# Two buffers instead of three for the transposed probabilities, four instead of two for the x tiles

## The reference, cut to what matters

```
h = max(layernorm(x), 0)
q = h @ Wq + bq;  k = h @ Wk + bk;  v = h @ Wv + bv        (8 heads of 64)
scores = q k^T / 8 + (adj == 0 ? -1e9 : 0)
x = x + softmax(scores) @ v
```

## Time and profile before

| | before |
|---|---|
| median of 3 runs | 4067.93 us (4066.05 to 4071.46) |
| the profiled execution | 4066.34 us |
| its span, first to last instruction | 4064.5 us |
| granted TensorE clock, mean | 0.999 |
| busy: PE / DVE / ACT / POOL | 4017.7 / 3064.8 / 3077.6 / 1401.6 us |
| batches x slots | 16 x 128 = 2048 |
| a slot, on average | 4064.5 / 2048 = 1.98 us |

### The profile page before, as it was taken

The page is one execution under the profiler, slowest core; times in us unless marked ns, Lnnn a source line. Parts: engine busy times, 40 slices in busy tenths (PEclk is TensorE's granted clock), DMA queues, the critical chain, the costliest instruction groups (busy, mean ns, idle before and its releaser), DMA issues. The chain is left out here.

```text
span 4064.5 us, 64393 instructions
## 1 busy us (share of the span) xinstructions
PE 4017.7 (99%) x22016; PEld 3277.6 (81%) x22016; DVE 3064.8 (75%) x5128; ACT 3077.6 (76%) x5514; POOL 1401.6 (34%) x1409
## 2 busy tenths in 40 slices
PE   7999999999999999999999999999999999999998
PEld 6888888888888888888888888888888888888886
DVE  6877867777777777777777687776877868768686
ACT  5877868778687786877868688686886868868687
POOL 4333333333333333333333333333333333333322
PEclk9999999999999999999999999999999999999999
DMA  5232223222223232222222232222322313223121
GB/s 183 69 93 63 85 59 84 86 65 83 70 72 86 66 85 80 62 83 80 74 81 64 78 92 61 81 79 64 93 66 77 85 59 91 83 59 98 38 73 47
DMA packets 239955, 314.83 MB, mean 77 GB/s; under 512 B 16401, under 2 KB 147473, under 8 KB 231057
## 3 DMA queue, kind: packets, MB, share of 16 engines
q1 hardware_dynamic: 239632, 310.71, 26.8%
HBM read 172.23 MB, written 37.75 MB: 52 GB/s over the span
## 5 line engine op out<-in xcount | busy, mean ns | idle before, releaser
L830 DVE TENSOR_TENSOR pT<-T,pT 128x512 fp32r<-128x512 f32 x2048 | 1390.7, 688 | 750.2 <-ACT pT L665 733.4
L665 ACT CAST pT<-T 128x512 fp32r<-128x512 f32 x2048 | 1186.1, 591 | 656.4 <-PE T L546 575.4
L824 DVE CUSTOM_DVE_ANT_0 S<-S,mask 128x1024 f32<-128x1024 f32 x1024 | 1252.1, 1223 | 3.1 <-PE S L535 3.1
L546 PE MATMUL T<-ident,probs 128*128 128x128 f32 x8192 | 1231.8, 273 | 1.0 <-ACT probs L673 0.6
L546 PEld LDWEIGHTS T<-ident,probs 128*128 128x128 f32 x8192 | 1006.6, 140 | 277.7 <-DVE pT L830 41.4
L673 ACT ACTIVATE probs<-S,negmax 128x1024 f32<-128x1024 f32 x1024 | 1151.5, 1124 | 8.4 <-DVE negmax L824 5.2
L565 PE MATMUL O<-pT,vs 128*64 128x512 f32 x2048 | 964.5, 471 | 0.2 <-DVE pT L830 0.2
L558 PE MATMUL O<-pT,vs 128*128 128x512 f32 x2048 | 816.1, 398 | 0.0
L504 PE MATMUL misc<-hT,wqk 128*128 128x512 f32 x3036 | 787.4, 395 | 7.7 <-ACT y L656 7.7
L504 PEld LDWEIGHTS misc<-hT,wqk 128*128 128x128 f32 x3036 | 556.9, 188 | 160.7 <-issue 42.9
L409 POOL TENSOR_TENSOR outs<-outs,oT 64x512 f32<-64x512 f32 x256 | 336.1, 1313 | 562.4 <-DMA outs<-oT 556.2
(11 more groups left out here) (70 smaller groups left out, 3587.5 us busy)
## 6 DMA issues: line engine op xcount, KB each, us to landing
wqk<-wqk_split SPq DMA_DIRECT2D x63, 1024.0 KB, 7.1
xln<-in_x SPq DMA_DIRECT2D x240, 256.0 KB, 2.7
outs<-in_x SPq DMA_DIRECT2D x66, 512.0 KB, 4.8
kA<-kA SPq DMA_DIRECT2D x128, 256.0 KB, 3.2
kB<-kB SPq DMA_DIRECT2D x128, 256.0 KB, 3.8
outs<-oT SPq DMA_DIRECT2D x256, 128.0 KB, 3.1
out<-outs SPq DMA_DIRECT2D x64, 512.0 KB, 4.4
probs<-in_adj SPq DMA_DIRECT2D x4, 1024.0 KB, 5.0
```

The lines of the kernel that those rows point to most:

```text
L546: mm = pe.transpose(T[:, u % 2, i * P:(i + 1) * P], probs[:, (GB * g + i) % RING, j * P:(j + 1) * P], ident[:])
L665: act.copy(pT[:, u % PT, 0, :], T[:, u % 2, :]).then_inc(p_hi, 1)
L824: dve.tensor_tensor_reduce(S[:, s % 2, :], S[:, s % 2, :], mask[:, s % NB, :], 1.0, 3.0e38, ALU.add, ALU.min, negmax[:, s % RING:s % RING ...
L830: dve.tensor_tensor(pT[:, u % PT, 1, :], T[:, u % 2, :], pT[:, u % PT, 0, :].bitcast(F32), ALU.subtract).then_inc(p_lo, 1)
```

## The change

`PT` goes from 3 to 2, so that pT has 8 KB a partition and not 12. `XLN` goes from 2 to 4, so that xln has 8 KB and not 4. With two buffers 128 is a multiple of the number of buffers, and the condition of `probs_hi` is the same in all slots: the `contract_lo` of u-2 must be done. No instruction is added or removed; the number of x loads is the same (16 a batch), four of them are issued at a batch's beginning and not two, and four and not six after transpositions.

```diff
-PT = 3
+PT = 2
...
-XLN = 2
+XLN = 4
 XLN_USES = [len(range(r, NB, XLN)) for r in range(XLN)]
...
                 n = UNITS * b + u
                 act.wait_ge(turned, n + 1)
 
-                used = n + 1 - (PT if u >= PT - 1 else PT - 1)
+                used = n + 1 - PT
                 if some(used):
                     act.wait_ge(contracted, used)
                 act.copy(pT[:, u % PT, 0, :], T[:, u % 2, :]).then_inc(p_hi, 1)
```

## The result

| | before | after |
|---|---|---|
| median | 4069.04 us (4066.05 to 4071.46) | 4323.23 us (4322.93 to 4324.79) |
| ratio, 95% interval | | 1.0626 (1.0607 to 1.0644): slower |
| span of the profiled execution | 4064.5 us | 4321.3 us |
| granted TensorE clock, mean | 0.999 | 0.999 |

The forecast was 4306 us, in a range of 4255 to 4400. By the spans (first to last instruction) the change cost 4321.3 - 4064.5 = 256.8 us; the sum had said 239.9.

What follows compares the result with a forecast made beforehand. PE, with only 12.7 us idle in its steady part, was taken to set the end. The terms 13.9 + 127.1 + 62.5 + 42.4 - 6 = 239.9 us, added to the profiled 4066.3 us, gave 4306 us, range 4255 to 4400.

Steps and rivals of the forecast that it cites:

- the sum: All terms of the forecast added up, four losses less the x tiles' gain: 239.9 us slower.
- The bound: PE's instruction list sets the end; it had 12.7 us idle, and a matmul that begins later is lost time.
- (b): Projections waiting for copy_y behind v = 10 and 2: PE stalls 1.65 or 1.33 us each, 127.1 + 62.5 us.
- (c): v = 18 and 26, no projection behind: the transposes two slots later start 0.53 us late in 80 places, 42.4 us.
- (a): Ordinary slots: probs_hi begins 0.29 us later, which costs only at the transposes of v = 17, 48 places, 13.9 us.
- Part 1, x tiles: Four x tiles end POOL's wait for loads; PE's waits at L483 shrink, a gain of 6 us, at most 15.0.
- the cover: At L483, most of a weight load's wait (10.4 us in all) is covered by the matmul beside it.
- The price of the wait: On ACT, probs_hi follows the end of the contract_lo it waits for by 0.09 us.
- The clock: Rival: PE's clock falls at the new gaps behind v = 2 and 10, up to 211 us more, 4517 us; chance 0.09.
- The loop without slack: Rival: the loop through ACT and DVE has no slack, so slots without fills lose 0.29 us, about 4636; chance 0.06.
- Not slower: Third rival: the wait is hidden at copy_y too and only the x tiles count, 4060 us; 0.04 with the fourth.

Runs made afterwards that it cites:

- experiment 1: The changed kernel with two x tile buffers (XLN = 2) in place of four: 4330.81 us, ratio to before 1.0644.
- experiment 4: The kernel before, with probs_hi waiting for contract_lo of u-2 in all slots but those with u mod 8 = 2: 4086.02 us, ratio 1.0041.
- experiment 3: The kernel before, with probs_hi's later wait only in slots with u mod 8 = 2 (and a batch's first two, as always): 4313.9 us, ratio 1.0602.
- experiment 5: The changed kernel, with ACT doing copy_y ahead of probs_hi in v = 2 and 10: 4135.18 us, ratio to before 1.016.
- experiment 7: The kernel before (three pT buffers, two x tiles), with copy_y between probs_hi and the exponential in v = 2 and 10: 4060.79 us, ratio 0.9981.

## Why the prediction was right, point by point

**The bound.** That PE's list sets the end held in every run: counted from the first instruction, the last matmul is 256.8 us late in the profile after, and the spans differ by 256.8; in each of the nine experiments' traces the two agree within 0.1 us too. The sum was 17.2 us short of 257.1: 7.7 in (b), 10.2 and 3.2 in places that it put at nothing and 0.2 in (c), less 2.1 in (a) and 2.0 at L483.

**Part 1, x tiles (-6 us).** The sign and the cover were right; the size was 8 us by matmul starts and 7.6 by medians of experiment 1. The step that was short is the cover of the weight loads' wait: PE's idle time came to 4.6 us in 8 places, but by matmul starts each of the 15 batches gained at L483, 0.2 to 1.9 us.

**The price of the wait (0.09 us).** It is 0.09 us again in the profile after, where `contract_lo` ends at 1965.72 and `probs_hi` begins at 1965.81.

**(a) Ordinary slots (13.9 us).** Measured 11.8 at v = 16 and 17, in the predicted pairs; experiment 4 has 12.0. But 7.2 of the 11.8 us stand one slot earlier than I said, at v = 16. The rows of after (ACT, DVE, PE):

```profile
1976.44 0.19 ACT L673 ACTIVATION_READ_ACCUMULATOR probs<-S,negmax 128x1 f32 x1
```

```profile
1975.99 0.66 DVE L830 TENSOR_TENSOR pT<-T,pT 128x512 fp32r<-128x512 f32 x1
```

```profile
1976.77 0.42 PEld L546 LDWEIGHTS T<-ident,probs 128*128 128x128 f32 x4 [0.39 <-ACT probs L673]
1976.80 0.63 PE L546 MATMUL T<-ident,probs 128*128 128x128 f32 x4
```

The transposes of v = 16 need both the exponential of v = 14, which ends at 1976.63, and `probs_low(14)`, which ends at 1976.65. Which of them is last can't be told from 0.02 us; the profile books the wait under the exponential, 40.9 us in 147 places, where it had 1.5 before. I had looked at `probs_low(15)` and v = 17 alone. The delay of 0.29 us is the same on all these ways, and what v = 16 takes, v = 17 need not take again, so the sum came out close all the same, in part by luck.

**(b) The projections (127.1 + 62.5 us).** Right in place, count and mechanism; experiments 3 and 5 show both. The term was mis-sized by 7.7 us of 189.6: v = 11 cost 1.75 us each and not 1.65. The first projection matmul is late by 1.67, as worked out. The rest is that the group itself lasts longer when it begins after a standstill: six matmuls show 1.62 us, and 1.54 when they follow without one. By the starts the difference lies between the first matmul and the second, 0.30 us apart and not 0.235; the cause is not shown. In the 47 places where the kernel before already waited, its group already showed 1.62, and there the term fits: 62.8 measured.

**(c) v = 20 and 28 (42.4 us).** Measured 42.6, but this is luck: two errors cancel. In the first, second and fourth pair a place cost 0.49 us, 39.2 in all, and not 0.53. The row of after has `probs_low` from 1982.09 to 1982.78 and the transposes at once:

```profile
1982.09 0.69 DVE L830 TENSOR_TENSOR pT<-T,pT 128x512 fp32r<-128x512 f32 x1 [0.69 <-ACT pT L665]
...
1982.83 0.66 PE L546 MATMUL T<-ident,probs 128*128 128x128 f32 x4 [0.23 <-DVE pT L830]
```

0.05 us lie between, where I took 0.15 from a place in which the weights were loaded first and the matmul then began beside them; part of that comes back as the slower start. The third pair, which I had left out with a bound of 17, cost 3.4.

**What the sum did not have.** 10.2 us at v = 18, 24 and 30, nearly all in the third pair, where the x transpositions stand. The prediction said that an x transposition leaves about nothing. That is near the truth for PE at v = 20, but the copies and differences that it brings with it lie on ACT and DVE, and the delay may come out later by them; no run separated this. Of the two halves of the wait, experiment 3 has the 4.2 us at v = 30, and experiment 4 has 3.3 at v = 18; of the 2.4 at v = 24, 1.3 come with the four x tiles (experiment 1).

**The rivals.** *The clock* did not fall at any gap. A stretch of after with a gap in it, as in the earlier trace rows:

```profile
1965.20:1968.60 3.40, 1.90 (x12) 1.39 (x11) 1.97 (x4) 2.79 (x6) 0.00 (x0) 1.00 0.20 42
```

1.90 us of work in 3.40, granted 1.00, and the steady part as a whole 1.00. Ahead of the fall in the kernel before it had been 1.48, but that row is no measure: in the profile after, the same stretch has 1.44 and no fall follows.

```profile
56.00:59.40 3.40, 1.44 (x7) 0.72 (x5) 2.23 (x4) 2.32 (x4) 0.41 (x1) 1.00 0.99 400
59.40:62.80 3.40, 1.85 (x7) 1.16 (x7) 2.48 (x4) 1.92 (x4) 0.00 (x0) 1.00 1.14 357
```

The Trainium skill tells of pauses between groups of matmuls that make the clock swing (TensorE: Matmul & The Clock Gate, "A second HAM failure mode: psum-queue depth-cycling"). The 124 pauses of this trace do not: it stays at 1.00.

*The loop without slack* fell by experiment 4. *Not slower*: it needed `copy_y` to end within 0.6 us of `contract_lo`; it ended 2.26 us after it. The third rival also leaned on the advice to double-buffer. In the Trainium skill (Trainium Kernel Development and Optimization, "Best Practices") that advice is about overlapping DMA with compute. pT is handed from engine to engine and no transfer touches it, so the advice says nothing of this buffer. Two buffers are enough in the 1792 slots of experiment 4 but for 17.5 us, and not where the releasing matmul stands last in its slot.

## What to carry to other kernels

The number of buffers says nothing until one knows where in the reader's program the release stands: here, by the trace of the kernel before, the second buffer comes free 0.28 us too late for `probs_hi` in the middle one of the ordinary slots, which cost little (17.5 us in all of them), and 0.9 to 1.9 us too late in one slot of eight, which cost 245. Look then at what is queued behind the waiting instruction on its engine; a copy that only shares the engine (`copy_y`) carried 197 of the 257 us. Before memory is spent on a transfer that comes late, look at what its queue does just before it: an order may give the same for nothing. And an engine without a pause is not yet an engine at its usual pace: compare the durations too.

## What the runs showed of the hardware

A group of matmuls that begins after a standstill of PE takes longer by itself: six of 512 columns show 1.62 us and 1.54 without one. The matmul starts put 1.75 us on a place whose first matmul was late by 1.67, so 0.08 us are added to the stall. The group shows the same 1.62 us behind 0.17 us of idle time as behind 1.50.

124 gaps of 1.5 us, with dense work on both sides, left the granted clock at 1.00.

DVE's differences for q (L807, 64 x 512, both operands in SBUF) were held beside POOL's add (L409): with two x tiles and `copy_y` moved (experiment 7), 63 of 63 that began during the add ended 0.55 us after it, in place of 0.69 us after their own start. DVE's instructions with an operand in PSUM were not: L830 kept 0.66 to 0.69 us and L824 its 1.22 beside the same add. No wait of the program ties the two.
